# A block of two feed-forward parts around delta-rule attention: the layer norm of the last two tiles moved ahead of a down layer, with unread products before it

## The chip, the cores and the metric

The kernel runs on one core of one Trainium2 chip. The time is what the device takes for one execution, in microseconds (us); where several executions were timed, their median is given. TensorE is called PE here, ScalarE ACT, VectorE DVE, GpSimd POOL.

## The reference

The input is 8 sequences of 256 tokens with 128 features. Three residual parts follow one another: half a feed-forward network (FFN), attention, and half the same FFN again.

```python
def ffn(x):                                   # w1, w2: 128 -> 512, h1, h2: 512 -> 512, w3: 512 -> 128, entries -1, 0, 1
    h = silu(lin(x, w1)) * lin(x, w2)
    h = gelu(lin(h, h1))
    h = gelu(lin(h, h2))
    return lin(h, w3)

x = x + 0.5 * ffn(layernorm(x))
x = x + attention(layernorm(x))               # ..., gates (softmax over 5 paths), weighted sum of the paths,
x = x + 0.5 * ffn(layernorm(x))               # an RMS norm over 32 channels, and a product with Wo
```

## The kernel before

All tokens lie along the free axis: x_t is 128 features x 2048 tokens, cut into four tiles of 512 tokens, and everything is written for tiles 0 to 3. A pair is two tiles: 0 and 1 first, 2 and 3 second. STEPS is one list of steps, written out by hand by `ffn_steps` and `att_steps`; every engine walks through this list in its own instruction stream, and the order in the list also numbers the PSUM banks. There are two rings of four banks of 128x512: ps_a, whose banks ACT frees (counted by the semaphore act_a), and ps_d, whose banks DVE frees (dve_d). A step that is the n-th user of ps_d waits until user n-4 has been freed, so the order of the list sets which bank waits for whom.

The change lies in the second FFN (f = 1 in the code), first pair, at its last hidden layer. The steps are:

- `up`: for each of four 128-row blocks m a product pair into ps_a (line 759, high part, and 760, low part) and one into ps_d; ACT takes Silu of the one (gbuf, L606), DVE multiplies by the other (hbuf, L1215), ACT copies it (L611) and DVE takes the rest (L1220).
- `hid1`, `hid2`: 8 products for each of four blocks m into ps_a; ACT applies Gelu twice (L631 and L634), DVE subtracts the rounded one from the exact one (L1241), so that the next layer has a high and a low part.
- `down`: 8 products into ps_d, then DVE adds the result to x (fin, L1191).
- `wo`: the output projection of the attention, one float32 product (L816), added to x_t by DVE (L1071). Tiles 2 and 3 have theirs inside the FFN's first pair, because the end of the attention's second half is worked off in the gaps of the first pair's hidden layers: the table FILL says behind which block which step of it is issued, on DVE or ACT. The last of it is a transpose on DVE (L1140).
- The norm of a tile: `mean` centres x by a float32 product with a constant matrix (L807), ACT squares it (L552), `var` averages the squares by another product (L812), ACT takes 1/sqrt (L558) and half its square (L561), DVE refines it by a Newton step (L1048, L1049, L1054) and splits the result into a high and a low part (xn, L1180 and L1182). Only then can `up` of this tile start.

ACT must load another table of functions when it goes from Gelu to 1/sqrt, back to Gelu, and to Silu. `preload` runs a one-element activation (L525), so that the load is done ahead of its use.

For tiles 2 and 3 the norm, and down of tile 0, are not walked through as steps of their own (`INNER`): each engine issues them inside `hid2` of tile 1, behind block m = 2. PE does so in `hidden`, ACT by `next_norm`, DVE in its hid2 branch. PE has ten more products behind them (L860), written to a bank that `up` overwrites, whose result nobody reads.

Of the kernel before, what the change touches and what calls it, by code (L numbers as in the profile page):

```python
# [32 lines left out]
def ffn_steps(f):  # L33
# [6 lines left out]
    for a in range(0, NT, 2):  # L40
# [8 lines left out]
        if more and last:  # L49

            s += [("hid1", f, a), ("hid1", f, b), ("hid2", f, a), ("wo", 2, 2), ("wo", 2, 3), ("hid2", f, b), ("down", f, a),
                  ("mean", f, 2), ("mean", f, 3), ("var", f, 2), ("var", f, 3)]
        elif more:
            s += [("scan", f, 2), ("hid1", f, a), ("mean", f, a + 2), ("mean", f, b + 2), ("flag", f, 2), ("hid1", f, b),
                  ("var", f, a + 2), ("var", f, b + 2), ("hid2", f, a), ("hid2", f, b)]
        elif last:
            s += [("out", f, 0), ("out", f, 1), ("hid1", f, a), ("hid1", f, b), ("hid2", f, a), ("hid2", f, b)]
        else:
            s += [("hid1", f, a), ("mean", 2, 0), ("mean", 2, 1), ("gsum", f, 1), ("hid1", f, b),
                  ("var", 2, 0), ("var", 2, 1), ("hid2", f, a), ("hid2", f, b)]  # L60
# [53 lines left out]
def before(kinds, weight=lambda s: 1):  # L114

    out, n = {}, 0
    for s in STEPS:
# [23 lines left out]
        ("hid1", 1, 3): [("add", 3)], ("hid2", 0, 0): [("osq", 2), ("rms", 1), ("scale", 1)], ("hid2", 0, 1): [("osq", 3)],  # L141
        ("hid2", 0, 3): [("wo", 2), ("wo", 3)]}
# [21 lines left out]
def program(nc, d, out):  # L164
    ctx = ExitStack()
    with ctx:
# [320 lines left out]
        def _(e):  # L487
# [75 lines left out]
            def next_norm():  # L563

                for s in NEXT_LN[0:2]:
                    mean(s)
                preload(ACT.Abs_reciprocal_sqrt)
                for s in NEXT_LN[2:4]:
                    var_(s)

            for s in STEPS:
# [50 lines left out]
                elif kind in ("hid1", "hid2"):  # L622
                    j = SET_AT[s]
                    set_free(e, j)
                    for m in range(KT):
# [12 lines left out]
                        if s == ("hid2", 1, 1) and m == 2:  # L638
# [93 lines left out]
        def _(e):  # L732
# [48 lines left out]
            def hidden(s, low):  # L781
# [4 lines left out]
                for m in range(KT):  # L786
# [8 lines left out]
                    if s == ("hid2", 1, 1) and m == 2:  # L795
                        wo(2)
                        wo(3)
                        down(("down", 1, 0), low)
                        for t in NEXT_LN[0:2]:
                            mean(t)  # L800
                        for t in NEXT_LN[2:4]:
                            var_(t)

# [23 lines left out]
            for s in STEPS:  # L827
# [24 lines left out]
                elif kind == "up":  # L852
# [5 lines left out]
                    if s == ("up", 1, 2):  # L858
                        for _ in range(10):
                            e.matmul(take_a(a)[:, :], w_f[1][:, 0:128], w_f[1][:, 0:512], start=True, stop=True)  # L860
# [142 lines left out]
        def _(e):  # L1003
# [191 lines left out]
            for s in STEPS:  # L1195
# [41 lines left out]
                elif kind in ("hid1", "hid2"):  # L1237
                    j = SET_AT[s]
                    for m in range(KT):
# [6 lines left out]
                        if s == ("hid2", 1, 1) and m == 2:  # L1246
                            down(("down", 1, 0))
                            for t in NEXT_LN[2:4]:
                                var_(t)
                    if s == ("hid2", 0, 1):  # L1250
# [159 lines left out]
```

## Time and profile before

| | us |
|---|---|
| median of 3 runs | 420.59 |
| lowest and highest of them | 418.59, 421.3 |
| the profiled execution, its own time | 419.48 |
| its span, from the first to the last instruction | 417.4 |

The profiled execution is one run beside those of the median; 2.08 us of its time lie outside its span. PE is busy for 360.7 us of the span, DVE for 306.0 and ACT for 272.7. The mean granted clock of TensorE is 0.918 of 2.4 GHz. Starts in the rows below are in us from the start of the span. Instructions of an engine overlap a little at their ends, so the next one can start before the printed end of the one ahead of it.

### The profile page before, as it was taken

Reading aid. Unit: us, or ns where it says so; the run is one execution under the profiler, and the core shown is the slowest. Engines: PE = TensorE matmul, PEld = TensorE weight load, DVE = VectorE, ACT = ScalarE, POOL = GpSimd, SP = SyncE. Lnnn points to the kernel's source line nnn. Section 1 sums busy time; section 2 is a strip of 40 time slices with the busy share of each in tenths; the row PEclk is TensorE's granted clock in tenths of the full one; section 3 lists DMA queues with packets and bytes.
Section 4 is the critical chain, followed back from the end, with each engine's and each line's share of the span. In section 5 each row is a group of like instructions: output and inputs, shape, how many; then the busy total and the mean of one; then the engine's idle time right before and its main releaser. Section 6 shows DMA issues by size and latency. Waiting matters only on the chain.

```text
span 417.4 us, 9821 instructions
## 1 busy us (share of the span) xinstructions
PE 360.7 (86%) x4132; PEld 272.7 (65%) x4132; DVE 306.0 (73%) x483; ACT 272.7 (65%) x429; POOL 54.2 (13%) x115
## 2 busy tenths in 40 slices
PE   7989999999999997799678389537799994999996
PEld 5767786777866775798567275423467762567885
DVE  2896578737648857999595969997857899597533
ACT  3888975879779886293433264516687844688873
POOL 5000000000012241201888300000000000000000
PEclk9999999999999998799856879656899999899999
DMA  8900006600000000071240000800000000001001
GB/s 283 329 2 2 2 2 195 160 2 2 2 0 0 1 3 2 12 221 54 66 114 8 2 5 2 270 12 2 0 2 2 2 2 1 2 2 50 3 2 50
DMA packets 14469, 19.49 MB, mean 47 GB/s; under 512 B 1104, under 2 KB 9296, under 8 KB 14416
## 3 DMA queue, kind: packets, MB, share of 16 engines
q1 hardware_dynamic: 14128, 18.68, 14.3%
q8 instruction: 44, 0.72, 0.7%
q14 instruction: 9, 0.07, 0.1%
q10 hardware_dynamic: 288, 0.02, 0.1%
HBM read 17.65 MB, written 1.05 MB: 45 GB/s over the span
## 4 chain that ended last, share of the span: by engine, by line
PE 54%; DVE 32%; ACT 7%; issue 5%; POOL 0%; DVEq 0%; ACTq 0%; POOLq 0%
PE ps_a L759 11%; PE ps_a L760 11%; PE ps_a L890 5%; DVE arena L1106 3%; DVE arena L1154 3%; PE ps_a L947 2%; DVE arena L1151 2%; PE ps_a L935 2%; DVE acts L1220 2%; PE ps_d L807 2%; PE ps_a L984 2%; PE ps_d L760 2%; PE ps_d L759 2%; PE ps_a L982 2%; DVE hbuf L1215 2%
## 5 line engine op out<-in xcount | busy, mean ns | idle before, releaser
L759 PE MATMUL ps_a<-acts,w_f 128*128 128x512 f32 x256 | 102.3, 400 | 3.8 <-ACT acts L634 2.2
L760 PE MATMUL ps_a<-acts,w_f 128*128 128x512 f32 x256 | 99.8, 390 | 0.0
L759 PEld LDWEIGHTS ps_a<-acts,w_f 128*128 128x128 f32 x256 | 48.0, 188 | 18.0 <-ACT acts L634 3.9
L760 PEld LDWEIGHTS ps_a<-acts,w_f 128*128 128x128 f32 x256 | 48.1, 188 | 10.3 <-issue 0.7
L634 ACT ACTIVATE acts<-ps_a,vec 128x512 fp32r<-128x512 f32 x64 | 44.5, 696 | 0.0
L1241 DVE TENSOR_TENSOR acts<-ghbuf,acts 128x512 fp32r<-128x512 f32 x32 | 21.2, 690 | 20.8 <-ACT acts L634 20.8
L1241 DVE TENSOR_TENSOR acts<-gbuf,acts 128x512 fp32r<-128x512 f32 x32 | 21.5, 688 | 17.4 <-ACT acts L634 17.4
L631 ACT ACTIVATE gbuf<-ps_a,vec 128x512 f32<-128x512 f32 x32 | 22.2, 695 | 14.1 <-DVE acts L1241 8.5
L890 PE MATMUL ps_a<-xnp,conv_w 128*128 128x512 f32 x108 | 27.3, 407 | 0.0
L631 ACT ACTIVATE ghbuf<-ps_a,vec 128x512 f32<-128x512 f32 x32 | 22.4, 699 | 7.1 <-PE ps_a L760 7.0
L935 PE MATMUL ps_a<-toep,arena 96*32 96x96 f32 x512 | 24.2, 356 | 0.0
L890 PEld LDWEIGHTS ps_a<-xnp,conv_w 128*128 128x128 f32 x108 | 20.3, 188 | 6.0 <-issue 1.4
L969 PE MATMUL ps_d<-arena 32*32 32x64 f32 x448 | 12.5, 269 | 13.1 <-DVE arena L1328 9.6
L935 PEld LDWEIGHTS ps_a<-toep,arena 96*32 96x32 f32 x512 | 20.0, 133 | 2.9 <-issue 1.6
L969 PEld LDWEIGHTS ps_d<-arena 32*32 32x32 f32 x448 | 9.7, 137 | 18.3 <-DVE arena L1328 11.7
L683 ACT ACTIVATE arena<-ps_a 128x384 f32<-128x384 f32 x16 | 7.8, 490 | 20.0 <-PE ps_a L935 20.0
L1048 DVE SCALAR_TENSOR_TENSOR arena<-ps_d,arena 128x512 f32<-128x512 f32 x16 | 11.0, 687 | 12.8 <-ACT arena L561 9.7
L477 POOL TENSOR_TENSOR arena<-arena 128x31 f32<-128x31 f32 (+15 forms) x31 | 15.7, 506 | 27.2 <-DVE arena L1300 24.9
L947 PE MATMUL ps_a<-arena 32*32 32x64 f32 x512 | 10.2, 247 | 8.6 <-DVE arena L1300 5.1
L759 PE MATMUL ps_a<-xn,w_f 128*128 128x512 f32 x32 | 14.4, 451 | 3.3 <-ACT low_any L615 0.9
L479 POOL TENSOR_TENSOR arena<-arena 128x31 f32<-128x31 f32 (+15 forms) x31 | 16.8, 541 | 2.4
L1215 DVE SCALAR_TENSOR_TENSOR hbuf<-ps_d,vec,gbuf 128x512 f32<-128x512 f32 x16 | 11.6, 748 | 6.9 <-ACT gbuf L606 4.1
(224 smaller groups left out, 799.8 us busy)
## 6 DMA issues: line engine op xcount, KB each, us to landing
toep<-in_fir SPq DMA_DIRECT2D x24, 288.0 KB, 5.9
w_in<-in_h SPq DMA_DIRECT2D x4, 1024.0 KB, 8.0
g_rows<-in_gW SPq DMA_DIRECT2D x4, 640.0 KB, 6.4
w_in<-in_w SPq DMA_DIRECT2D x6, 256.0 KB, 4.4
iobuf<-in_x SPq DMA_DIRECT2D x4, 256.0 KB, 5.8
y<-iobuf SPq DMA_DIRECT2D x3, 256.0 KB, 2.2
toep<-in_taps SPq DMA_DIRECT2D x1, 512.0 KB, 5.7
toep<-in_proj SPq DMA_DIRECT2D x1, 256.0 KB, 8.1
```

What stands on the lines that cost most here:

```text
L477: own(e.tensor_tensor(prod, lmat[1][:, j + 1:DH, j:j + 1].to_broadcast(shape), tinv[1][:, j:j + 1, 0:j + 1].to_broadcast(shape), ALU.mult))
L479: own(e.tensor_tensor(sub, sub, prod, ALU.subtract))
L631: e.activation(gbuf[f][:, gi % 4], src[:, :], ACT.Gelu, scale=sc).then_inc(S["act_step"], 1)
L634: e.activation(acts[f][:, j % 3, 0, m], src[:, :], ACT.Gelu, scale=sc).then_inc(S["act_a"], 1)
L759: e.matmul(bank, w, hi, start=start, stop=False)
L760: return e.matmul(bank, w, lo, start=False, stop=stop)
L890: last = e.matmul(bank, conv_w[:, hw, ww], xnp[:, hx, 2 * i:2 * i + 2, o:o + L], start=n == 0, stop=n == len(todo) - 1)
L935: last = e.matmul(bank[32 * h:32 * h + 32, WIN * c4:WIN * c4 + WIN], vt[half][0:WIN, DH * h + 8 * grp + dl, :], toep[0:WIN, grp % 2, h, :, ...
L947: last = e.matmul(bank[r, 64 * n:64 * n + 64], xt[r, g, h, n], vk[r, g, h, n].rearrange("p x c -> p (x c)"), start=True, stop=True)
L969: last = e.matmul(bank[r, 64 * b:64 * b + 64].rearrange("p (x t) -> p x t", x=2), s_sb[r, g, b], aqs[g][r, b, n], start=True, stop=True)
L1215: e.scalar_tensor_tensor(out=hbuf[f][:, m % 2], in0=ps_d[:, (dd + m) % NRING], scalar=vc("s2", m), in1=gbuf[f][:, (KT * j + m) % 4], op0=A ...
L1241: e.tensor_tensor(acts[f][:, j % 3, 1, m], gbuf[f][:, (KT * j + m) % 4], acts[f][:, j % 3, 0, m].bitcast(F32), ALU.subtract).then_inc(S["d ...
```

## The change

In the list of steps down of tile 0 now stands behind the norm of tiles 2 and 3, which renumbers the ps_d banks: the order of users was wo 2, wo 3, down 0, mean 2, mean 3, var 2, var 3, and is wo 2, wo 3, mean 2, mean 3, var 2, var 3, down 0.

PE: behind block 2 of hid2 of tile 1 it issues twelve unread products into the bank of block 3, then the two output projections, then the norm's four products; block 3 and then down of tile 0 follow. The ten unread products ahead of `up` of tile 2 are gone.

ACT: `next_norm` comes behind block 1 of hid2 of tile 1, no longer behind block 2, and the table of 1/sqrt is loaded ahead of the two squares, no longer behind them.

DVE: the sums of wo 2 and wo 3 are issued behind blocks 1 and 2 of hid2 of tile 0, no longer both behind block 3; the norm's refinement comes behind block 1 of hid2 of tile 1; down of tile 0 behind its block 3.

```diff
@@ ffn_steps
-            s += [("hid1", f, a), ("hid1", f, b), ("hid2", f, a), ("wo", 2, 2), ("wo", 2, 3), ("hid2", f, b), ("down", f, a),
-                  ("mean", f, 2), ("mean", f, 3), ("var", f, 2), ("var", f, 3)]
+            s += [("hid1", f, a), ("hid1", f, b), ("hid2", f, a), ("wo", 2, 2), ("wo", 2, 3), ("hid2", f, b),
+                  ("mean", f, 2), ("mean", f, 3), ("var", f, 2), ("var", f, 3), ("down", f, a)]
@@ FILL
-        ("hid1", 1, 3): [("add", 3)], ("hid2", 0, 0): [("osq", 2), ("rms", 1), ("scale", 1)], ("hid2", 0, 1): [("osq", 3)],
-        ("hid2", 0, 3): [("wo", 2), ("wo", 3)]}
+        ("hid1", 1, 3): [("add", 3)], ("hid2", 0, 0): [("osq", 2), ("rms", 1), ("scale", 1)], ("hid2", 0, 1): [("osq", 3), ("wo", 2)],
+        ("hid2", 0, 2): [("wo", 3)]}
@@ scalar: next_norm
+                preload(ACT.Abs_reciprocal_sqrt)
                 for s in NEXT_LN[0:2]:
                     mean(s)
-                preload(ACT.Abs_reciprocal_sqrt)
                 for s in NEXT_LN[2:4]:
                     var_(s)
@@ scalar: hid1, hid2
-                        if s == ("hid2", 1, 1) and m == 2:
+                        if s == ("hid2", 1, 1) and m == 1:
                             next_norm()
@@ tensor: hidden
                     if s == ("hid2", 1, 1) and m == 2:
+                        for _ in range(12):
+                            e.matmul(take_a(a + 3)[:, :], w_f[1][:, 0:128], w_f[1][:, 0:512], start=True, stop=True)
                         wo(2)
                         wo(3)
-                        down(("down", 1, 0), low)
                         for t in NEXT_LN[0:2]:
                             mean(t)
                         for t in NEXT_LN[2:4]:
                             var_(t)
+                if s == ("hid2", 1, 1):
+                    down(("down", 1, 0), low)
@@ tensor: up
-                    if s == ("up", 1, 2):
-                        for _ in range(10):
-                            e.matmul(take_a(a)[:, :], w_f[1][:, 0:128], w_f[1][:, 0:512], start=True, stop=True)
@@ vector: hid1, hid2
-                        if s == ("hid2", 1, 1) and m == 2:
-                            down(("down", 1, 0))
+                        if s == ("hid2", 1, 1) and m == 1:
                             for t in NEXT_LN[2:4]:
                                 var_(t)
+                    if s == ("hid2", 1, 1):
+                        down(("down", 1, 0))
```

On DVE, from the transpose that ends the attention to the first refinement of the norm, the one order stands against the other like this (L1241 is the subtraction of a hidden block, L1071 the sum of an output projection, L1191 down, L1048 and L1049 the refinement):

```order
 L1135 TENSOR_TENSOR arena<-arena 128x1024
 L1140 STREAM_TRANSPOSE arena<-arena 128x32x32
+L1241 TENSOR_TENSOR acts<-gbuf,acts 128x512
+L1071 TENSOR_TENSOR x_t<-x_t,ps_d 128x512
+L1241 TENSOR_TENSOR acts<-gbuf,acts 128x512
+L1071 TENSOR_TENSOR x_t<-x_t,ps_d 128x512
 L1241 TENSOR_TENSOR acts<-gbuf,acts 128x512 x3
-L1071 TENSOR_TENSOR x_t<-x_t,ps_d 128x512 x2
-L1241 TENSOR_TENSOR acts<-gbuf,acts 128x512 x3
-L1191 SCALAR_TENSOR_TENSOR fin<-ps_d,vec,x_t 128x512
 L1048 SCALAR_TENSOR_TENSOR arena<-ps_d,arena 128x512
 L1049 SCALAR_TENSOR_TENSOR arena<-ps_d,arena 128x512
```

The two sums moved ahead by two and by one subtraction, and one subtraction and down have left the stretch. They stand behind the norm now, ahead of the first product with the gate (L1215):

```order
 L1180 CAST xn<-arena 128x512
 L1182 TENSOR_TENSOR xn<-arena,xn 128x512
-L1241 TENSOR_TENSOR acts<-gbuf,acts 128x512
+L1241 TENSOR_TENSOR acts<-gbuf,acts 128x512 x2
+L1191 SCALAR_TENSOR_TENSOR fin<-ps_d,vec,x_t 128x512
 L1215 SCALAR_TENSOR_TENSOR hbuf<-ps_d,vec,gbuf 128x512 x2
 L1220 TENSOR_TENSOR acts<-hbuf,acts 128x512
```

Between the norm of tile 3 and the gate products DVE had one instruction of the first pair, and has three.

On ACT, the stretch around the norm, before (L631 and L634 are the Gelus of one block, L525 the table and the one-element activation, L552 the squares, L558 and L561 1/sqrt and the square of it):

```order
L631 ACTIVATE gbuf<-ps_a,vec 128x512
L634 ACTIVATE acts<-ps_a,vec 128x512
L552 ACTIVATE arena<-ps_d 128x512 x2
L525 ACT_TABLE_LOAD
L525 ACTIVATE vec<-vec 128x1
L558 ACTIVATE arena<-ps_d,vec 128x512
```

and of the change, the same stretch, where the table stands ahead of the squares, right behind the Gelus of block 1:

```order
L631 ACTIVATE gbuf<-ps_a,vec 128x512
L634 ACTIVATE acts<-ps_a,vec 128x512
L525 ACT_TABLE_LOAD
L525 ACTIVATE vec<-vec 128x1
L552 ACTIVATE arena<-ps_d 128x512 x2
L558 ACTIVATE arena<-ps_d,vec 128x512
```

## Rows read from the trace of the kernel before

**Rows 1.** The page's part 4: shares by engine of the chain that ended last.

```profile
PE 54%; DVE 32%; ACT 7%; issue 5%; POOL 0%; DVEq 0%; ACTq 0%; POOLq 0%
```

**Rows 2.** The chain that ended last, in order of time: start us, us, what.

```profile
359.18 1.73 PE ps_d L807 x4
...
361.61 1.28 ACT L525
...
377.03 0.76 DVE fin L1191
```

**Rows 3.** Timeline of PE: start us, us, instruction, idle before it and its releaser.

```profile
347.85 0.50 PE L759 MATMUL ps_a<-acts,w_f 128*128 128x512 f32 x1 [1.81 <-ACT acts L634]
...
353.85 3.49 PE L816 MATMUL ps_d<-arena,wo_w 128*128 128x512 f32 x4 [3.88 <-DVE arena L1140]
...
359.01 1.88 PE L807 MATMUL ps_d<-x_t,cent_w 128*128 128x512 f32 x4
...
362.20 0.79 PE L759 MATMUL ps_a<-acts,w_f 128*128 128x512 f32 x1
...
364.46 2.43 PE L860 MATMUL ps_a<-w_f 128*128 128x512 f32 x10
367.64 0.50 PE L759 MATMUL ps_a<-xn,w_f 128*128 128x512 f32 x1 [0.75 <-DVE xn L1182]
...
368.93 0.47 PE L759 MATMUL ps_a<-xn,w_f 128*128 128x512 f32 x1
```

**Rows 4.** Timeline of ACT, the same columns.

```profile
354.41 0.69 ACT L631 ACTIVATE gbuf<-ps_a,vec 128x512 f32<-128x512 f32 x1 [4.29 <-DVE acts L1241]
...
360.13 0.60 ACT L552 ACTIVATE arena<-ps_d 128x512 f32<-128x512 f32 x1 [3.31 <-PE ps_d L807]
...
362.90 0.20 ACT L525 ACTIVATE vec<-vec 128x1 f32<-128x1 f32 x1
363.01 0.67 ACT L558 ACTIVATE arena<-ps_d,vec 128x512 f32<-128x512 f32 x1
363.72 0.63 ACT L561 ACTIVATE arena<-arena 128x512 f32<-128x512 f32 x1
...
366.90 0.69 ACT L631 ACTIVATE gbuf<-ps_a,vec 128x512 f32<-128x512 f32 x1
...
369.59 1.25 ACT L606 ACTIVATE gbuf<-ps_a,vec 128x512 f32<-128x512 f32 x2
```

**Rows 5.** Timeline of DVE, the same columns.

```profile
353.64 1.85 DVE L1241 TENSOR_TENSOR acts<-gbuf,acts 128x512 fp32r<-128x512 f32 x3
355.96 0.69 DVE L1071 TENSOR_TENSOR x_t<-x_t,ps_d 128x512 f32<-128x512 f32 x1 [0.47 <-PE ps_d L816]
357.37 0.69 DVE L1071 TENSOR_TENSOR x_t<-x_t,ps_d 128x512 f32<-128x512 f32 x1 [0.72 <-PE ps_d L816]
...
364.38 0.69 DVE L1048 SCALAR_TENSOR_TENSOR arena<-ps_d,arena 128x512 f32<-128x512 f32 x1 [3.86 <-ACT arena L561]
...
367.50 0.68 DVE L1048 SCALAR_TENSOR_TENSOR arena<-ps_d,arena 128x512 f32<-128x512 f32 x1
...
370.61 0.69 DVE L1241 TENSOR_TENSOR acts<-gbuf,acts 128x512 fp32r<-128x512 f32 x1
371.22 1.40 DVE L1215 SCALAR_TENSOR_TENSOR hbuf<-ps_d,vec,gbuf 128x512 f32<-128x512 f32 x2
...
377.69 1.40 DVE L1215 SCALAR_TENSOR_TENSOR hbuf<-ps_d,vec,gbuf 128x512 f32<-128x512 f32 x2
```

**Rows 6.** Windows: PE, PEld, DVE, ACT, POOL busy, clock, DMA, GB/s.

```profile
345.60:350.00 4.40, 2.55 (x10) 1.42 (x8) 3.96 (x13) 3.99 (x7) 0.00 (x0) 1.00 0.00 2
350.00:353.40 3.40, 0.00 (x0) 0.00 (x0) 3.26 (x5) 0.11 (x1) 0.00 (x0) 1.00 0.00 0
353.60:356.80 3.20, 2.95 (x5) 1.41 (x5) 2.59 (x5) 2.39 (x4) 0.00 (x0) 0.50 0.00 0
380.00:412.00 32.00, 32.00 (x142) 26.38 (x142) 15.09 (x22) 24.05 (x39) 0.00 (x0) 1.00 0.06 18
```

## The prediction

> **What bounds the kernel now.** I read the shares of the chain that ended last first: more than half of it is PE, a third DVE [rows 1]. So the kernel has no single bound, and an edit is worth what it takes out of the chain in its own stretch. There the chain runs, as the timelines show, through these links: DVE's transpose releases the output projection on PE after 3.88 us of idling (353.85), PE does two projections, down of tile 0 and the two means; ACT squares, loads a table and takes 1/sqrt; DVE refines tile 2 from 364.38 and tile 3 from 367.50, subtracts one hidden block and starts the gate products of `up` at 371.22 [rows 2 to 5]. From there DVE and ACT hand each other the blocks of `up` until fin at 377.03, and from 380 to 412 PE is busy for 32.00 of 32.00 us [rows 2, 6]. The reader is to see that the tail behind 371.22 holds no slack: what DVE's start of `up` gains, the end gains, if nothing in `up` changes in order. Nothing ahead of 350 is touched.
>
> A second thing to see is the clock. PE's granted clock is 1.00 from 350.0 to 353.4, in which PE does nothing, and 0.50 (1.2 GHz) from 353.6 to 356.8, exactly under the two projections [rows 6]. Those four passes took 3.49 us; the four passes of the two means, the same shape in float32, took 1.73 at full clock, 0.43 each [rows 2, 3].
>
> **The twelve unread products.** They follow block 2 of hid2, which starts at 347.85. Eight products of it at 0.24 us (ten unread ones took 2.43 [rows 3]) end near 349.8, and twelve more take 2.9, until 352.7. The bank that they write was freed by then: ACT is through tile 0's Gelus and waits for DVE until 354.41 [rows 4]. The projection can't start before 353.85, when the transpose lets it go, so they cost nothing, with 1.1 us to spare. PE's idling shrinks from 3.88 to about 1.1 us. An idling of 1.81 us at 347.85 left the clock at 1.00 [rows 3, 6], so I take the full clock for the projections. Each product is two passes; at 1.2 GHz a pass takes 0.85, at 2.4 GHz 0.43. The first product let DVE go at 355.96, now 0.85 earlier, at 355.1. The second, 0.86 behind, is done at 356.0, where DVE had it at 357.37 [rows 5].
>
> **Down of tile 0 leaves the path, the sums move ahead.** DVE sums tile 2 from 355.1 to 355.8, subtracts block 2 until 356.3 (a step of 0.6, as 370.61 to 371.22 [rows 5]), and sums tile 3 until 357.0. The mean of tile 2 starts at 355.8, not 359.01 [rows 3]. It took 1.12 us from its start until ACT had it (359.01 to 360.13 [rows 3, 4]), so it is there at 356.9; the mean of tile 3 starts at 357.05 and is there at 358.2.
>
> **The table ahead of the squares.** ACT's two Gelus of block 1 start at 354.41 as before, since DVE's first subtraction behind the transpose, which releases them, has not moved [rows 4, 5]. They end at 355.7. Table 1.28 and one-element activation 0.20 (with its overlap, 1.4 together, from 361.61 to 363.01 [rows 2, 4]) end at 357.1. Hence the square of tile 2 runs from 357.1 to 357.7 and that of tile 3 from 358.2 to 358.8. Ahead of it the load cost the path 1.4 us; now it lies beside the mean, and only 0.2 us of it are left. The product of var 2 starts behind the mean of tile 3, at 358.0, and is there 1.1 later, at 359.1. 1/sqrt takes 0.71 and the square 0.66 until DVE begins (363.01, 363.72, 364.38 [rows 4, 5]): DVE begins at 360.4. That is 4.0 us earlier than 364.38.
>
> The Trainium skill ("ScalarE: Activation LUTs", What ACT_TABLE_LOAD costs) prices a switch of tables at the load and a drain of 1.38 us beside it, 2.66 us in all. The rows show the load's 1.28 and the next activation right behind it, and no such drain ahead of it; by the page's price the square of tile 2 would wait until 358.4 and the gain would shrink by about 1.2 us. I go by the rows.
>
> **What it gives back.** DVE is in order, and from its first refinement on it has no gap. Before, the gate products stood behind two refinements (3.12 and 3.11) and one subtraction (0.61). Now blocks 2 and 3 are both subtracted behind them, and down of tile 0 is added: 3.12 + 3.11 + 0.61 + 0.61 + 0.66 (fin to the next instruction, 377.03 to 377.69 [rows 2, 5]) = 8.11 us. DVE reaches the gate products at 360.4 + 8.1 = 368.5, against 371.22: **2.7 us earlier**. So 1.3 of the 4.0 are paid back.
>
> **Is something else late at 368.5?** ACT: the squares of tile 3's norm end at 361.7; Gelu's table 1.28, two blocks of Gelus 2.4 (two of 0.69 less overlap each), Silu's table and the one-element activation 1.4 give 366.8 for the first Silu, against 369.59 [rows 4]. It needs 0.7 us, so DVE is still the last, by 1.0 us. PE: the products of var 3 end near 359.9, block 3 and down of tile 0 are 16 products at 0.23, until 363.6. The first product of `up` would then be free to go with xn of tile 2 at 363.5. But the bank order has changed: `up`'s first block takes in ps_d the bank of mean 3, which the refinement of tile 3 frees. Before, the second block did, and started 1.43 us behind that refinement's start (367.50 to 368.93 [rows 3, 5]). Now the first starts at 363.5 + 1.4 = 364.9, 2.7 before 367.64, and is done a full microsecond ahead of ACT's Silu. Block 3 of `up` waits for the bank of down, freed at 368.5; DVE wants that block 3.7 us behind its first. Hidden as well.
>
> **The ten unread products that go.** They filled 364.46 to 366.9, in front of an idle stretch of 0.75 us [rows 3]. Without them PE idles 1.3 us there and under 1 us ahead of `up`'s block 3, shorter than the 1.81 that kept the clock. Their price is 0; if the clock fell all the same, `up`'s 16 products would take 0.43 each instead of 0.23, 3.2 us more on PE, of which DVE's pace hides about two: a loss of up to 1.4.
>
> **The sum.** Before, 10.5 us pass from the projection's start to DVE's first refinement (353.85 to 364.38). Now it is 1.25 (first projection) + 0.7 + 0.6 + 0.65 (sum, subtraction, sum) + 0.95 (mean of tile 3) + 1.1 (var 2) + 0.71 + 0.66 (1/sqrt, square) = 6.6, so 3.9 to 4.0 less. With 1.3 given back on DVE that is **-2.7 us**. The profiled execution took 419.48 and would take 416.8. Its time is 1.1 below the median of the three runs, inside their scatter of 2.7; against the median I forecast 420.59 - 2.7 = **417.9 us**. About 1% (4.2 us) is what a measurement of this kernel can tell from no change, so this is a gain within 1%.
>
> **Rivals.**
> 1. The clock is at 1.2 GHz under the projections all the same. For it: PE does little useful before. Against it: the 1.81 us gap. Then DVE sums tile 3 at 357.4 to 358.1, its mean is there at 359.2, var 2 at 360.1, DVE begins at 361.5: 2.9 - 1.3 = 1.6 gained, **419.0**. The same time, within 0.5 us, follows where the switch of tables costs a drain: the first DVE refinement at 361.6 and 419.1.
> 2. The lead of the norm carries through in full, 4.0 us: **416.6**. That needs DVE's three extra instructions to find a gap. It idles for 1.6 us ahead of the first refinement (three subtractions from 357.0 on end at 358.8), but there the Gelus of blocks 2 and 3 don't exist yet, so the order speaks against it.
> 3. The change doesn't do what it says: the unread products hold up the projection. At 1.2 GHz twelve take 5.1 us, until 354.9, and the projection starts 1.1 late on top of the first rival: **420.1**. The clock of 1.00 over 345.6 to 353.4 speaks against it.
> 4. Slower: the clock falls behind 364, where ten products kept PE busy and now don't. One fall like the one of 353.6 to 356.8 costs the path at most half of 3.2 us, 1.6 [rows 6]. It takes over 5.4 us at 1.2 GHz on PE's own path to eat the 2.7. Two such falls in the stretch behind 377, where PE sets the pace, give 3.2 - 2.7 = +0.5, **421.1**; beyond that each adds 1.6. That stretch is busy throughout, which speaks against it.
>
> **How the numbers follow.** The forecast 0.72 (its own range 416.6 to 419.2, 1.3 either way as the scatter of the three runs), rival 1 with the drain 0.14, rival 2 0.08, rival 3 0.03, rival 4 0.03. The range of 416.2 to 419.7 takes in the first three, with the scatter. Faster by over 1% means 416.4 or less: half of rival 2 and about a tenth of the forecast, 0.12. Slower by over 1%, 424.8 or more, is the far end of rival 4 alone, 0.01 to 0.02. The rest, 0.86, is within 1%.
>
> **What would show it.** Right: twelve L797 products between 349.8 and 352.8; the projections' four passes in under 2.1 us at a clock of 1.00; the table load (L525) near 355.7, ahead of the squares; L1048 of tile 2 near 360.4; `up`'s first product at 364.9 released by DVE's refinement and not by xn; the first L1215 near 368.5; fin of tile 1 near 374.3; the span near 414.7. Wrong: if DVE waits between its refinements and the gate products, ACT's two tables and four Gelus, of which I leave 1.0 us of margin, have become the late ones; if PE's first product of block 3 of `up` is what DVE waits for, the bank order was mispriced.

## The result, and the profile after

The changed kernel takes 416.63 us in the median of 8 runs (415.76 to 418.74), the kernel before beside it 420.38 (8 runs, 418.55 to 421.56). The ratio estimated from all these runs is 0.9924, with a 95% interval from 0.9895 to 0.9953: faster by 3.2 us, or 2.0 to 4.4. (The two medians alone would give 0.9911.) Single executions that were clearly longer than the others of their kernel are left out of the ratios here and below. The profiled execution of the changed kernel has a span of 414.8 us, 2.6 less than before. The shares of the chain that ended last, from part 4 of the page of the profile, differ from [rows 1] by two points more on DVE and one less on ACT:

```profile
PE 54%; DVE 34%; ACT 6%; issue 5%; POOL 0%; DVEq 0%; ACTq 0%; POOLq 0%
```

PE's timeline of the stretch (start us, us, instruction, idle before it and its releaser) answers to [rows 3]:

```profile
349.90 2.89 PE L797 MATMUL ps_a<-w_f 128*128 128x512 f32 x12
353.98 1.98 PE L819 MATMUL ps_d<-arena,wo_w 128*128 128x512 f32 x4 [1.19 <-DVE arena L1140]
355.89 2.32 PE L810 MATMUL ps_d<-x_t,cent_w 128*128 128x512 f32 x4
358.05 2.04 PE L815 MATMUL ps_d<-arena,mean_w 128*128 128x512 f32 x4
...
365.04 0.47 PE L759 MATMUL ps_a<-xn,w_f 128*128 128x512 f32 x1 [1.10 <-DVE arena L1049]
...
368.82 0.47 PE L759 MATMUL ps_a<-xn,w_f 128*128 128x512 f32 x1 [0.81 <-DVE fin L1191]
```

The twelve unread products (L797) end 1.19 us before the projection may start. The projections' four passes take 1.98 us where they took 3.49. The means start right behind them and take 2.32 us, 0.44 more than before, since the second has to wait for DVE's sum of tile 3 (356.35). `up`'s first product is released by the refinement of tile 3 (L1049), no longer by xn: the price of the new bank order. ACT's timeline, against [rows 4]:

```profile
355.12 0.68 ACT L634 ACTIVATE acts<-ps_a,vec 128x512 fp32r<-128x512 f32 x1
355.82 1.28 ACT L525 ACT_TABLE_LOAD   x1
357.12 0.20 ACT L525 ACTIVATE vec<-vec 128x1 f32<-128x1 f32 x1
357.23 0.58 ACT L552 ACTIVATE arena<-ps_d 128x512 f32<-128x512 f32 x1
358.31 0.60 ACT L552 ACTIVATE arena<-ps_d 128x512 f32<-128x512 f32 x1 [0.50 <-PE ps_d L810]
359.11 0.69 ACT L558 ACTIVATE arena<-ps_d,vec 128x512 f32<-128x512 f32 x1 [0.20 <-PE ps_d L815]
...
366.86 1.25 ACT L606 ACTIVATE gbuf<-ps_a,vec 128x512 f32<-128x512 f32 x2
```

The table load starts right behind the Gelus of block 1 and ends beside the means. The first mean would have let its square go 1.12 us behind its own start, at 357.01 (as with no unread products, 355.87 to 356.99), so the table holds the square up by 0.2 us; the second square waits 0.50 us for PE. The load starts 0.02 us behind the end of the Gelus, and the next activation 0.02 us behind the load's own end. With the price that the Trainium skill gives for a switch of tables ("ScalarE: Activation LUTs", What ACT_TABLE_LOAD costs: a drain of 1.38 us beside the load), which the prediction weighed, this trace disagrees. DVE's timeline, against [rows 5]:

```profile
355.14 0.69 DVE L1071 TENSOR_TENSOR x_t<-x_t,ps_d 128x512 f32<-128x512 f32 x1 [0.70 <-PE ps_d L819]
...
356.35 0.68 DVE L1071 TENSOR_TENSOR x_t<-x_t,ps_d 128x512 f32<-128x512 f32 x1
...
360.49 0.69 DVE L1048 SCALAR_TENSOR_TENSOR arena<-ps_d,arena 128x512 f32<-128x512 f32 x1 [1.65 <-ACT arena L561]
...
366.72 1.29 DVE L1241 TENSOR_TENSOR acts<-gbuf,acts 128x512 fp32r<-128x512 f32 x2
367.93 0.75 DVE L1191 SCALAR_TENSOR_TENSOR fin<-ps_d,vec,x_t 128x512 f32<-128x512 f32 x1
368.59 1.40 DVE L1215 SCALAR_TENSOR_TENSOR hbuf<-ps_d,vec,gbuf 128x512 f32<-128x512 f32 x2
```

The first refinement came 3.89 us earlier (360.49 for 364.38), the second 3.12 us behind it as before (363.61), and the first gate product (L1215) 2.63 us earlier (368.59 for 371.22): between them stand two subtractions and a fin (L1191) where one subtraction stood. The windows (PE, PEld, DVE, ACT and POOL busy, granted clock, DMA share, GB/s) answer to [rows 6]:

```profile
350.00:353.40 3.40, 2.79 (x13) 1.96 (x11) 3.23 (x5) 0.20 (x1) 0.00 (x0) 1.00 0.00 0
353.60:356.80 3.20, 2.82 (x6) 0.97 (x6) 2.50 (x5) 2.24 (x3) 0.00 (x0) 1.00 0.00 0
377.00:412.00 35.00, 34.20 (x155) 27.89 (x153) 16.07 (x24) 25.38 (x42) 0.00 (x0) 1.00 0.06 16
```

PE is busy for 2.79 of the 3.40 us in which it did nothing before, and its clock is 1.00 under the projections, where it was 0.50. From 377 to 412 it is busy for 34.20 of 35.00 us; before it was 34.11 in the same window.

### The profile page after: what moved, and what is told of

Its sections match the earlier page's. It is cut to its first block, busy times and chain, and to the rows that moved or that the text cites. A ratio compares the mean times of both kernels' runs of the same rounds, so it can differ in the third digit from the quotient of the medians.

```text
span 414.8 us, 9825 instructions
## 1 busy us (share of the span) xinstructions
PE 360.7 (87%) x4134; PEld 270.7 (65%) x4134; DVE 306.3 (74%) x483; ACT 272.8 (66%) x429; POOL 54.2 (13%) x115
## 3 DMA queue, kind: packets, MB, share of 16 engines
HBM read 17.65 MB, written 1.05 MB: 45 GB/s over the span
## 4 chain that ended last, share of the span: by engine, by line
PE 54%; DVE 34%; ACT 6%; issue 5%; POOL 0%; DVEq 0%; ACTq 0%; POOLq 0%
PE ps_a L759 12%; PE ps_a L760 11%; PE ps_a L890 5%; DVE arena L1154 3%; DVE arena L1106 3%; DVE arena L1151 3%; PE ps_a L947 2%; PE ps_a L935 2%; PE ps_a L984 2%; DVE acts L1220 2%; PE ps_d L957 2%; PE ps_d L810 2%; PE ps_a L982 2%; DVE hbuf L1215 2%; PE ps_d L760 1%
## 5 line engine op out<-in xcount | busy, mean ns | idle before, releaser
L634 ACT ACTIVATE acts<-ps_a,vec 128x512 fp32r<-128x512 f32 x64 | 44.5, 695 | 0.0
L1241 DVE TENSOR_TENSOR acts<-ghbuf,acts 128x512 fp32r<-128x512 f32 x32 | 21.2, 689 | 20.7 <-ACT acts L634 20.7
L1241 DVE TENSOR_TENSOR acts<-gbuf,acts 128x512 fp32r<-128x512 f32 x32 | 21.6, 689 | 17.5 <-ACT acts L634 17.4
L631 ACT ACTIVATE gbuf<-ps_a,vec 128x512 f32<-128x512 f32 x32 | 22.2, 695 | 14.2 <-DVE acts L1241 8.5
L631 ACT ACTIVATE ghbuf<-ps_a,vec 128x512 f32<-128x512 f32 x32 | 22.4, 699 | 7.1 <-PE ps_a L760 7.1
L935 PEld LDWEIGHTS ps_a<-toep,arena 96*32 96x32 f32 x512 | 18.6, 130 | 4.7 <-issue 1.9
L1048 DVE SCALAR_TENSOR_TENSOR arena<-ps_d,arena 128x512 f32<-128x512 f32 x16 | 11.0, 687 | 10.3 <-ACT arena L561 7.5
L1215 DVE SCALAR_TENSOR_TENSOR hbuf<-ps_d,vec,gbuf 128x512 f32<-128x512 f32 x16 | 11.6, 748 | 6.9 <-ACT gbuf L606 4.1
L947 PE MATMUL ps_a<-arena 32*32 32x64 f32 x512 | 9.3, 234 | 8.0 <-DVE arena L1301 4.7
```

The costliest lines, as they stand in the source:

```text
L631: e.activation(gbuf[f][:, gi % 4], src[:, :], ACT.Gelu, scale=sc).then_inc(S["act_step"], 1)
L634: e.activation(acts[f][:, j % 3, 0, m], src[:, :], ACT.Gelu, scale=sc).then_inc(S["act_a"], 1)
L935: last = e.matmul(bank[32 * h:32 * h + 32, WIN * c4:WIN * c4 + WIN], vt[half][0:WIN, DH * h + 8 * grp + dl, :], toep[0:WIN, grp % 2, h, :, ...
L947: last = e.matmul(bank[r, 64 * n:64 * n + 64], xt[r, g, h, n], vk[r, g, h, n].rearrange("p x c -> p (x c)"), start=True, stop=True)
L1215: e.scalar_tensor_tensor(out=hbuf[f][:, m % 2], in0=ps_d[:, (dd + m) % NRING], scalar=vc("s2", m), in1=gbuf[f][:, (KT * j + m) % 4], op0=A ...
L1241: e.tensor_tensor(acts[f][:, j % 3, 1, m], gbuf[f][:, (KT * j + m) % 4], acts[f][:, j % 3, 0, m].bitcast(F32), ALU.subtract).then_inc(S["d ...
```

## The experiments

A profile's positions can be compared closely only from a common point, because what lies ahead of the projections differs from run to run: over the fourteen profiles they start between 351.16 and 355.16 us. So the table counts from the start of the projections (P) to DVE's first refinement, to the first gate product, and to the end of the span. With 24 unread products the start itself is late; there P is put at the end of DVE's transpose (353.05) plus the 0.05 us that lie between the two in the change. P is the start of the row `ps_d<-arena,wo_w` on PE; the refinement and the gate product are the first rows `arena<-ps_d,arena` and `hbuf<-ps_d,vec,gbuf` behind it on DVE. Line numbers in the rows move by a few from kernel to kernel.

| kernel | P | refinement | gate product | end | ratio of the timed runs to before |
|---|---|---|---|---|---|
| before | 353.85 | 10.53 | 17.37 | 63.55 | |
| the change | 353.98 | 6.51 | 14.61 | 60.82 | 0.9924 [0.9895, 0.9953] |
| the change again | 355.16 | 6.51 | 14.61 | 60.84 | 0.9933 [0.9897, 0.9969] |
| change, no unread products | 352.67 | 7.54 | 15.64 | 61.83 | 0.9967 [0.9942, 0.9991] |
| change, 5 | 353.06 | 9.04 | 17.13 | 63.34 | 0.9955 [0.9922, 0.9987] |
| change, 5, again | 353.90 | 9.04 | 17.14 | 63.40 | 0.9976 [0.9944, 1.0008] |
| change, 24 | 353.10 | 7.62 | 15.72 | 61.90 | 0.9953 [0.9924, 0.9982] |
| change, table behind the squares | 353.69 | 7.71 | 15.80 | 62.01 | 0.9949 [0.9918, 0.9979] |
| change, down ahead of the means | 354.79 | 8.59 | 16.02 | 62.21 | 0.9945 [0.9920, 0.9969] |
| change, ten products back | 354.96 | 6.51 | 14.61 | 60.84 | 0.9936 [0.9906, 0.9967] |
| before, twelve products | 351.16 | 9.04 | 15.87 | 62.14 | 0.9917 [0.9887, 0.9946] |
| before, twelve products, again | 351.76 | 9.03 | 15.86 | 62.04 | 0.9948 [0.9920, 0.9977] |
| before, twelve products and early table | 353.14 | 7.98 | 14.82 | 61.06 | 0.9941 [0.9911, 0.9972] |
| a version with less on DVE | 354.60 | 6.51 | 14.00 | 60.20 | 0.9900 [0.9869, 0.9932] |

The same kernel, run and profiled again, has the same distances within 0.1 us. The timed ratios have intervals of some 0.3% to each side, 1.2 us. They can't rank the variants by themselves: what is said below of parts and variants rests on one or two profiles each.

The distances leave one small thing out, because they start behind DVE's transpose. It takes 1.91 us in the kernel before, with no unread products and with five, 1.96 us with twelve, and 2.09 us with 24. Counted from the transpose's start, the change gains 2.72 us and not 2.76. Why the transpose is slower beside a busy PE wasn't tried.

**The change without its unread products.**

```diff
                     if s == ("hid2", 1, 1) and m == 2:
-                        for _ in range(12):
-                            e.matmul(take_a(a + 3)[:, :], w_f[1][:, 0:128], w_f[1][:, 0:512], start=True, stop=True)
                         wo(2)
```

> The changed kernel without the twelve unread products; everything else as changed. My theory: they are worth what the clock gives. PE idles some 4 us ahead of the output projections again, the four passes run at 1.2 GHz (clock 0.50 in that window) and take about 3.5 us instead of 1.98. DVE's second sum then starts near 357.4 instead of 356.35, its first refinement near 361.6 instead of 360.49 and the first gate product (L1215) near 369.7 instead of 368.59: 1.1 us slower than the changed kernel, ratio to the kernel before 0.996. Rival: the order alone gives the gain and the clock hides behind ACT's table load: the first gate product stays within 0.3 us of 368.6, ratio 0.993.

PE's timeline and windows of this kernel:

```profile
352.67 3.37 PE L817 MATMUL ps_d<-arena,wo_w 128*128 128x512 f32 x4 [3.87 <-DVE arena L1138]
```

```profile
349.00:352.00 3.00, 0.00 (x0) 0.00 (x0) 2.90 (x4) 0.00 (x0) 0.00 (x0) 1.00 0.00 0
353.00:355.00 2.00, 2.00 (x3) 0.83 (x3) 0.36 (x2) 1.76 (x3) 0.00 (x0) 0.50 0.00 0
356.00:358.00 2.00, 2.00 (x6) 0.69 (x5) 2.00 (x5) 0.60 (x2) 0.00 (x0) 1.00 0.00 0
```

PE idles 3.87 us, the clock falls to 0.50, the four passes take 3.37 us, and the gate product is 1.03 us later than in the change. The first theory holds, to 0.1 us; the clock is on the path.

**The unread products alone.** The same loop of twelve, put into the kernel before, with nothing else changed.

> The kernel before with one addition: the twelve unread products ahead of the output projections; down stays between projections and means, the table behind the squares, and the ten later products stay. My theory: the projections run at 2.4 GHz, DVE's second sum starts near 355.95 instead of 357.37, the first refinement near 363.0 instead of 364.38, and nothing is given back on DVE: 1.4 us faster than the kernel before, ratio 0.997. Rival (the clock is not on the path there): first refinement within 0.3 us of 364.4, ratio 1.000.

The projections on PE and the gate product on DVE:

```profile
351.16 1.98 PE L818 MATMUL ps_d<-arena,wo_w 128*128 128x512 f32 x4 [1.21 <-DVE arena L1142]
...
367.03 1.40 DVE L1217 SCALAR_TENSOR_TENSOR hbuf<-ps_d,vec,gbuf 128x512 f32<-128x512 f32 x2
```

The four passes take 1.98 us and everything behind comes 1.5 us earlier than before (15.87 for 17.37), as expected. But the timed ratio, 0.9917, says 3.5 us, and its interval ends below the 0.9966 that 1.4 us would give. Its attention part had ended 2.7 us earlier than that of the kernel before (P 351.16), though the instructions there are the same. So the kernel was run again.

> The kernel before with the twelve unread products, unchanged from its first run, which was faster in the timed runs (0.9917) than its stretch in the trace explains (1.4 us, 0.9966). Theory A: the surplus is chance of the attention's stretch, whose clock differs from run to run; now the ratio lies between 0.994 and 0.999. Theory B: the surplus belongs to the kernel; the ratio is again under 0.994 and its attention is again 2 us and more ahead of the kernel before.

The ratio was 0.9948 and the attention again ended early, 2.1 us ahead of before. The ratio fits theory A, the position theory B; the stretch repeats to 0.01 us. Whether the early attention belongs to this kernel stays open. It arises mostly between 152 and 222 us, where both profiles of this kernel gain 2.3 us on that of the kernel before. The profile of the change gains 1.9 us there and its repetition 0.2, so such a lead isn't bound to this kernel alone. By the timed runs alone (0.9917 and 0.9948) the twelve products in the kernel before can't be told from the whole change (0.9924 and 0.9933).

**The table back behind the squares.**

```diff
             def next_norm():
 
-                preload(ACT.Abs_reciprocal_sqrt)
                 for s in NEXT_LN[0:2]:
                     mean(s)
+                preload(ACT.Abs_reciprocal_sqrt)
```

> The changed kernel with the table of 1/sqrt loaded behind the two squares, as before the change. My theory: the squares run at 357.0 and 358.3, the load from 358.9, and 1/sqrt of tile 2 starts near 360.35 instead of 359.11: 1.2 us later all the way to the first gate product (369.8), ratio 0.996. Rival (a switch of tables costs a drain besides the load, wherever it stands): the shift is 1.3 us plus another 1.4, first gate product near 371.2.

ACT's timeline of this kernel:

```profile
358.01 0.60 ACT L552 ACTIVATE arena<-ps_d 128x512 f32<-128x512 f32 x1 [0.60 <-PE ps_d L810]
358.63 1.28 ACT L525 ACT_TABLE_LOAD   x1
...
360.03 0.67 ACT L558 ACTIVATE arena<-ps_d,vec 128x512 f32<-128x512 f32 x1
```

Square, load and 1/sqrt follow without a gap but for the one element's 0.1 us, the refinement is 1.20 and the gate product 1.19 us later than in the change. The first theory holds; the drain of the rival would have shown as a gap of 1.4 us ahead of or behind the load, and there is none where the load stands here or in the change.

**Down of tile 0 back ahead of the means.**

```diff
-            s += [("hid1", f, a), ("hid1", f, b), ("hid2", f, a), ("wo", 2, 2), ("wo", 2, 3), ("hid2", f, b),
-                  ("mean", f, 2), ("mean", f, 3), ("var", f, 2), ("var", f, 3), ("down", f, a)]
+            s += [("hid1", f, a), ("hid1", f, b), ("hid2", f, a), ("wo", 2, 2), ("wo", 2, 3), ("hid2", f, b), ("down", f, a),
+                  ("mean", f, 2), ("mean", f, 3), ("var", f, 2), ("var", f, 3)]
...
                         wo(3)
+                        down(("down", 1, 0), low)
...
-                if s == ("hid2", 1, 1):
-                    down(("down", 1, 0), low)
...
                         if s == ("hid2", 1, 1) and m == 1:
+                            down(("down", 1, 0))
                             for t in NEXT_LN[2:4]:
                                 var_(t)
-                    if s == ("hid2", 1, 1):
-                        down(("down", 1, 0))
```

> The changed kernel with down of tile 0 put back between the output projections and the means, on PE, on DVE (ahead of the refinement) and in the order of the banks; unread products, early table and early sums as changed. My theory: eight products of down cost the means 1.85 us less the 0.15 that they waited, the first refinement starts near 362.0 instead of 360.49, but DVE has down done ahead of it and reaches the first gate product 7.45 us later instead of 8.1: near 369.5, 0.9 us slower than the changed kernel, ratio 0.9945. Rival (the bank of the third mean is what holds `up` back, and its old order frees it): the first gate product within 0.3 us of 368.6, ratio 0.993.

PE's timeline of this kernel:

```profile
358.49 0.50 PE L759 MATMUL ps_d<-acts,w_f 128*128 128x512 f32 x1 [0.34 <-DVE acts L1240]
...
359.06 1.88 PE L809 MATMUL ps_d<-x_t,cent_w 128*128 128x512 f32 x4
...
366.63 0.50 PE L759 MATMUL ps_a<-xn,w_f 128*128 128x512 f32 x1 [1.96 <-DVE xn L1181]
```

The gate product came 1.41 us later than in the change, not 0.9. From refinement to gate product DVE took 7.43 us, as expected; the missing half microsecond lies ahead. The last two products of down waited for DVE's subtraction of block 3, which the early sums of tiles 2 and 3 had pushed back: PE idled 0.34 us ahead of them (358.49). The means start 4.27 us behind P, where in the two kernels that keep both down and the late sums (351.16 and 353.14 in the table) they start at 3.67. So with down on the path the early sums cost 0.6 us. Neither theory had this wait.

**The ten later products back.** The loop of ten that the change removed ahead of `up` of tile 2 is put back.

> The changed kernel with the ten unread products ahead of `up` of tile 2 put back. My theory: they run from about 363.8 to 366.1, `up`'s first product starts 1.1 us later than 365.04 and is done near 367.1, before ACT's first Silu ends its own queue (366.86) by little: the first gate product at 368.6 to 368.7, ratio 0.9925, the same as the changed kernel. Rival (their removal is part of the gain): the first gate product later by a microsecond or more, ratio 0.995 and up.

```profile
364.76 2.43 PE L863 MATMUL ps_a<-w_f 128*128 128x512 f32 x10
367.02 0.39 PE L759 MATMUL ps_a<-xn,w_f 128*128 128x512 f32 x1
```

With them `up`'s first product starts 1.0 us later, counted from P (12.06 for 11.06), and DVE's gate product stands at 14.61, as in the change. The first theory holds: removing them was free and gained nothing.

**Twenty-four and five unread products**, in place of twelve: `range(24)` and `range(5)` in the loop.

> The changed kernel with twenty-four unread products ahead of the output projections instead of twelve. My theory: the twelve have 1.2 us to spare, so twelve more (2.7 us) push the projections from 353.98 to 355.4 and everything behind by 1.4 to 1.5 us: first gate product near 370.1, ratio 0.996. Rival (more products make the clock surer and cost nothing): same time as the changed kernel.

PE's timeline of this kernel, with DVE's transpose between:

```profile
348.88 5.60 PE L797 MATMUL ps_a<-w_f 128*128 128x512 f32 x24
350.96 2.09 DVE L1140 STREAM_TRANSPOSE arena<-arena 128x1024 f32<-128x1024 f32 x1
354.32 1.88 PE L819 MATMUL ps_d<-arena,wo_w 128*128 128x512 f32 x4
```

PE goes from the 24 products, 0.227 us each, into the projections without idling. They start 1.22 us behind P, and the gate product comes 1.1 us later than in the change; expected were 1.4 to 1.5. Counted from the start of the transpose, which takes 2.09 us here for 1.96 in the change, it is 1.24 us. The first theory holds: the spare time of the twelve was real, and twice as many use it up.

> The changed kernel with five unread products instead of twelve: PE then idles 2.9 us ahead of the output projections, between the 1.8 us that left the clock at full and the 3.9 us that didn't. Theory A (any idling under 3 us is safe here): four passes in under 2.1 us, ratio 0.9925. Theory B (a longer gap lowers the clock in part of the runs or of the stretch): passes of 0.85 us, first gate product up to 1.1 us later, ratio up to 0.996.

The windows of this kernel, then those of its second run:

```profile
350.40:352.10 1.70, 0.00 (x0) 0.00 (x0) 1.67 (x2) 0.00 (x0) 0.00 (x0) 1.00 0.00 0
352.40:359.10 6.70, 6.04 (x7) 2.42 (x8) 4.63 (x8) 3.21 (x5) 0.00 (x0) 0.50 0.00 0
359.50:361.00 1.50, 1.50 (x4) 0.49 (x3) 0.00 (x0) 0.88 (x2) 0.00 (x0) 1.00 0.06 11
```

```profile
353.50:360.00 6.50, 6.10 (x7) 2.42 (x8) 4.44 (x8) 3.26 (x5) 0.00 (x0) 0.50 0.00 0
360.10:362.00 1.90, 1.90 (x7) 0.73 (x5) 0.12 (x1) 1.04 (x2) 0.00 (x0) 1.00 0.03 9
```

The gate product of the first of the two runs:

```profile
370.19 1.40 DVE L1215 SCALAR_TENSOR_TENSOR hbuf<-ps_d,vec,gbuf 128x512 f32<-128x512 f32 x2
```

PE idled for 2.74 us, the clock fell at 352.4, and it stayed at 0.50 for some 6.8 us: under the projections and under the means too. The gate product came 2.5 us later than in the change and 1.5 later than with no unread product at all. I had given this 1.1 us at most, so it was run again:

> The changed kernel with five unread products, unchanged from its first run, in which PE's clock was 0.50 for 6.9 us from 352.3 on, twice as long as with none. Theory A (where the fall and the return of the clock lie differs from run to run): this time the four passes and the means cost 0 to 1.1 us more than in the changed kernel. Theory B (five products are in themselves worse than none): again 2.5 us more, first gate product 17.1 us behind the start of the projections.

Theory B, by the profiles: 17.14 and 17.13. The timed runs (0.9955 and 0.9976) don't tell five products from none (0.9967).

**The two cheap parts together.** The kernel before with the loop of twelve and the `preload` ahead of the squares.

> The kernel before with two of the change's parts: the twelve unread products ahead of the output projections, and the table of 1/sqrt loaded ahead of the squares. Down, the sums and the norm's place on ACT and DVE stay as before, and so do the ten later products. My theory: the table fits in while PE does down and the means, counted from the start of the projections the first refinement comes at 8.0 (10.53 before, 9.04 with the products alone, 6.51 in the change) and the first gate product at 14.8 (17.37, 15.87, 14.61). So nearly the whole gain is had without moving down: ratio 0.9935 to 0.994. Rival (the second block of Gelus ahead of the table keeps the squares waiting): first refinement at 8.6 or later, gate product at 15.5, ratio 0.9955.

ACT's timeline of this kernel, and DVE's gate product:

```profile
356.14 1.28 ACT L525 ACT_TABLE_LOAD   x1
...
357.93 0.60 ACT L552 ACTIVATE arena<-ps_d 128x512 f32<-128x512 f32 x1 [0.29 <-PE ps_d L809]
...
359.74 0.69 ACT L558 ACTIVATE arena<-ps_d,vec 128x512 f32<-128x512 f32 x1 [0.36 <-PE ps_d L814]
...
367.96 1.40 DVE L1217 SCALAR_TENSOR_TENSOR hbuf<-ps_d,vec,gbuf 128x512 f32<-128x512 f32 x2
```

Here ACT does the Gelus of block 2 as well ahead of the table, and the table is still done 0.29 us before the first mean lets the square go. The refinement stands at 7.98 and the gate product at 14.82; expected were 8.0 and 14.8, so the first theory holds. This kernel, without the move of down, is 0.21 us behind the change.

**A version with less on DVE.** What the change gives back lies on DVE, behind the norm, while DVE idles 1.65 us ahead of it. This version moves a subtraction into that gap. ACT does block 2's Gelus ahead of the table, which leaves it no time for the second square ahead of 1/sqrt; DVE takes that square over. The two sums of the projections go back by one block each.

```diff
 FILL:
-        ... ("hid2", 0, 1): [("osq", 3), ("wo", 2)],
-        ("hid2", 0, 2): [("wo", 3)]}
+        ... ("hid2", 0, 1): [("osq", 3)],
+        ("hid2", 0, 2): [("wo", 2)], ("hid2", 0, 3): [("wo", 3)]}
 scalar:
-                preload(ACT.Abs_reciprocal_sqrt)
-                for s in NEXT_LN[0:2]:
-                    mean(s)
+                mean(NEXT_LN[0])
+                preload(ACT.Abs_reciprocal_sqrt)
...
-                        if s == ("hid2", 1, 1) and m == 1:
+                        if s == ("hid2", 1, 1) and m == 2:
                             next_norm()
 vector:
                         if s == ("hid2", 1, 1) and m == 1:
+                            t = D_AT[NEXT_LN[1]]
+                            e.wait_ge(S["pe_d"], t + 1)
+                            e.wait_ge(S["act_sq"], NORM_AT[NEXT_LN[0]] + 1)
+                            own(e.tensor_copy(lnb[1]["sq"][:, 1], ps_d[:, t % NRING]))
+                            settle()
+                            e.tensor_tensor(lnb[1]["sq"][:, 1], lnb[1]["sq"][:, 1], ps_d[:, t % NRING], ALU.mult).then_inc(S["act_sq"], 1)
+                        if s == ("hid2", 1, 1) and m == 2:
                             for t in NEXT_LN[2:4]:
                                 var_(t)
```

> A version meant to take back part of what DVE gives back. From the changed kernel: ACT does the Gelus of block 2 of hid2 of tile 1 ahead of the table load, DVE subtracts block 2 in its idle time ahead of the first refinement, ACT squares tile 2 only (ahead of the table) and DVE squares tile 3 (a copy and a product); DVE subtracts block 2 of tile 0 ahead of the first sum. My theory: the first refinement stays at 360.5, the gate products begin 0.6 us earlier, near 368.0, ratio 0.991, 0.6 us under the changed kernel. Rival: ACT, with a block of Gelus more ahead of the table, brings 1/sqrt later than 359.11 by 0.6 us or more, and nothing is gained.

DVE's timeline of this kernel:

```profile
358.87 0.69 DVE L1249 COPY arena<-ps_d 128x512 f32<-128x512 f32 x1
359.59 0.69 DVE L1251 TENSOR_TENSOR arena<-arena,ps_d 128x512 f32<-128x512 f32 x1
360.20 0.68 DVE L1240 TENSOR_TENSOR acts<-gbuf,acts 128x512 fp32r<-128x512 f32 x1
361.11 0.69 DVE L1047 SCALAR_TENSOR_TENSOR arena<-ps_d,arena 128x512 f32<-128x512 f32 x1 [0.23 <-ACT arena L561]
...
367.34 0.68 DVE L1240 TENSOR_TENSOR acts<-gbuf,acts 128x512 fp32r<-128x512 f32 x1
367.94 0.74 DVE L1190 SCALAR_TENSOR_TENSOR fin<-ps_d,vec,x_t 128x512 f32<-128x512 f32 x1
368.60 1.40 DVE L1214 SCALAR_TENSOR_TENSOR hbuf<-ps_d,vec,gbuf 128x512 f32<-128x512 f32 x2
```

Its idling ahead of the refinement is 0.23 us, the refinement stands at 6.51, and one subtraction instead of two follows the norm: the gate product at 14.00, 0.61 us ahead of the change, and the end 0.62 ahead. The timed ratio, 0.990, is the lowest of all, but its interval doesn't tell it from the change. It is the fastest version by its trace.

**The last run** was the change once more, beside three of these kernels:

> The changed kernel once more, on the chip and beside the runs of the two above. Both theories: ratio 0.9935 by the 2.7 us of its stretch, within 0.003; first gate product 14.6 us behind the start of the projections.

The ratio was 0.9933 and the gate product stood at 14.61.

## Why the prediction was right

*The clock under the projections.* Right. The passes took 1.98 us (under 2.1 was foretold) at a clock of 1.00. Alone the twelve products gain 1.5 us, and taking them out of the change costs 1.0; rival 1 had put that at 1.1. The step that led there, that an idling of up to 1.81 us is safe, held for the 1.19 us here. But the length of the idling alone doesn't settle it: with down put back the clock fell behind one of 1.96 us, and only 1.2 us after PE had resumed.

*The twelve cost nothing, with 1.1 us to spare.* Right but for 0.05 us in the transpose beside them: 1.19 us are left over. With 24 the spare time is used up and the rest, 1.1 us, appears at the end.

*The table.* Right in its place and price: 355.82 for 355.7 foretold, 0.2 us of it left on the path, 1.2 us in the change when it is put back, 1.05 us in the kernel before (15.87 to 14.82). The drain of rival 1's second half didn't happen.

*Down leaves the path, and DVE gives back 1.3.* Right: refinement 3.89 us earlier for the 3.9 to 4.0 of the sum, 8.10 us from there to the gate product for 8.1, so 1.26 given back. The two cheap parts show what that means: down's move with its companions (the sums and the norm ahead by a block) brings the refinement 1.47 us forward and pays 1.26 of it back. Added in this order to the kernel before, the products bring 1.50 us, the table 1.05 and down's move 0.21, together 2.76. Taken one at a time out of the finished change, they are worth 1.03, 1.19 and, for down's move alone, 1.41: together 3.6, so the parts overlap, and no split of the 2.76 holds by itself. The prediction didn't say this of the parts, and its sum doesn't show it, because it went from start to end in one chain.

*Who is late next.* Right: `up`'s first product at 365.04 (364.9 foretold), released by the refinement of tile 3; ACT's first Silu at 366.86 (366.8), and with 0.7 us for it 1.0 us is left before DVE wants it, as foretold; fin of tile 1 at 374.39 (374.3); the span 414.8 (414.7).

*The ten products.* Right, 0.00 us.

*The rivals.* The whole lead of 4.0 (rival 2) was not had, although its time of 416.6 is nearer to the measured 416.63 than the forecast's 417.9: the trace decides here, with 1.26 us given back, and not the time; a subtraction can be moved into the gap that its text called unusable, but only by giving ACT's Gelus of block 2 a place ahead of the table, and it is worth 0.6. The products didn't hold up the projection (rival 3). Rival 4 asked for falls of the clock behind 364 on PE's path. The two profiles of the change show none (1.00 throughout). One fall came with down put back, where PE had idled 1.96 us ahead of `up`; the clock was 0.50 in this window of it:

```profile
368.00:370.00 2.00, 2.00 (x5) 1.61 (x6) 1.93 (x4) 1.97 (x4) 0.00 (x0) 0.50 0.00 0
```

DVE went on at its own pace there: from the gate product to the end pass 46.19 us, and 46.21 in the change. So it cost nothing.

*The time.* 417.9 was foretold and 416.63 measured, 1.3 us less, inside the range. By the stretch the gain is 2.7 us of the measured 3.2, or 2.8 in the repeated runs (0.9933); the rest is within the intervals. That the time alone came out within 1.3 us is in part luck, because the base matters as much as the sum: the median of three runs stood at 420.59, that of the same kernel in the later runs at 418.87 to 420.38.

## What to carry to other kernels

Price the parts of a change one by one and in the kernel before as well: here, by the profiles, a loop of unread products and one moved line gave 2.55 of 2.76 us, and the rearrangement that looks like the change added 0.21 to them, because an engine that works without a gap from the norm on had to do the moved work all the same. Price them from the other side too, by taking each out of the finished change: here the worths came out otherwise (1.03, 1.19 and 1.41). The unread products were worth it where they ended just short of the wait and kept the clock; 24 delayed the work, and five cost more than none in both profiles. And where a gain is below a half per cent, compare distances from a common point of two traces, not the timed medians alone. Such a distance says nothing of what lies ahead of the point, as the early attention of the kernel with the products alone shows.

## What the runs showed of the hardware

An idling of 2.74 us behind five unread products brought TensorE's clock to 1.2 GHz in both profiles, for some 6.8 us (352.4 to 359.2 and 353.2 to 360.1). After 3.87 us of plain idling, with no products, it was low for 3.4 us (352.1 to 355.5), and after 3.88 us in the kernel before for as long (353.5 to 356.9). Behind an idling of 1.96 us it fell once, 1.2 us after PE had resumed, and stayed low for 3.4 us. Behind idlings of 1.19 us (the change) and 1.81 us (the kernel before) it stayed at 2.4 GHz. So the length of the idling alone doesn't say whether and for how long the clock falls. What of the 2.74 us makes the low stretch twice as long wasn't tried.

The start of the projections moved by 4.0 us between profiles of kernels that are the same up to there. By 31 us from the start of the span the profiles are already up to 1.5 us apart; from there to 152 us, at a granted clock of 1.00, the fourteen profiles keep their distances to 0.1 us. The rest comes in the attention, between 152 and 323 us, in steps of up to 2.3 us; from 323 to the transpose ahead of the projections the profiles run in parallel to 0.04 us. The steps go with the granted clock. From the transpose at 296.8 us to the one at 323.3, seven profiles take 26.5 to 26.6 us at a mean clock of 0.94, and the other seven take 24.9 at 1.00. Between 261.5 and 290.7 it is the other way round: the first seven take 29.2 to 29.5 us at 0.59 or 0.60, the other seven 30.5 to 30.6 at 0.55. From 246.9 to 261.5, seven take 14.6 to 15.0 us at 1.00, and seven take 16.0 to 16.9 at 0.89 or 0.90. So much of the scatter in the attention is which of these falls of the clock an execution meets. What decides it wasn't tried.
